# Four units of the next A pass scored ahead, and B's head in other banks

## The reference

```
x = x + attn_a(layernorm(x))   # 16 heads of 8, over the 256 positions, with a bias table by distance
x = x + ffn(layernorm(x))      # one shared expert, and 7 routed ones of which each token takes the best 2
x = x + attn_b(layernorm(x))   # 16 heads of 8, over the 32 sequences at one position, output projection
x = x + ffn(layernorm(x))      # same weights again
```

## Time and profile before

| | us |
|---|---|
| median of 3 runs | 2579.62 (2575.34 to 2588.03) |
| the profiled execution | 2579.83 |
| its span in the trace | 2578.0 |
| TensorE, VectorE, ScalarE, POOL busy | 2069.0, 1596.0, 1358.8, 881.0 |

### The profile page before, as it was taken

How to read it: one execution, slowest core, us unless ns; L and a number is a source line. 1 busy time by engine, 2 the same in 40 slices (tenths; PEclk the granted TensorE clock), 3 DMA queues, 4 the chain that set the end, 5 groups by cost and what they waited for, 6 DMA issues and landing times. The chain is left out here.

```text
span 2578.0 us, 51329 instructions
## 1 busy us (share of the span) xinstructions
PE 2069.0 (80%) x14166; PEld 1400.4 (54%) x14166; DVE 1596.0 (62%) x6106; ACT 1358.8 (53%) x2893; POOL 881.0 (34%) x953
## 2 busy tenths in 40 slices
PE   5789999999999999949999656767676676599995
PEld 3456666666666666626665444545545454366663
DVE  3477777777777777736555346565656655355552
ACT  3577888888888888715444332323223232154442
POOL 3111111111111111126777612222231313177776
PEclk8788888888888888869999867676777777699998
DMA  5100000000000000036777511101010100377774
GB/s 199 56 16 15 16 17 17 17 17 17 17 17 17 17 17 17 14 110 155 178 178 169 110 30 32 31 29 33 25 37 25 33 25 25 128 160 176 181 175 81
DMA packets 125947, 168.85 MB, mean 65 GB/s; under 512 B 17288, under 2 KB 93968, under 8 KB 125888
## 3 DMA queue, kind: packets, MB, share of 16 engines
q1 hardware_dynamic: 62400, 122.50, 15.0%
q0 software_dynamic: 51968, 37.26, 9.8%
q10 hardware_dynamic: 11520, 8.39, 1.2%
HBM read 111.96 MB, written 56.12 MB: 65 GB/s over the span
## 5 line engine op out<-in xcount | busy, mean ns | idle before, releaser
L1092 ACT ACTIVATE z<-z,nm 128x256 f32<-128x256 f32 x1024 | 440.2, 500 | 94.1 <-DVE nm L1342 93.8
L1342 DVE CUSTOM_DVE_ANT_0 z<-bank_S,big 128x256 f32<-128x256 f32 x1024 | 378.9, 420 | 166.8 <-PE bank_S L1615 127.8
L961 POOL DMA_INDIRECT sent<-rows,slots x256 | 249.2, 973 | 243.2 <-DVE slots L1425 167.1
L1502 DVE SCALAR_TENSOR_TENSOR both<-both,bank_E 128x512 f32<-128x512 f32 (+1 forms) x228 | 155.5, 682 | 227.1 <-ACT both L1162 226.7
L1031 POOL DMA_INDIRECT out_x<-yo,xs x152 | 236.1, 1553 | 119.8 <-ACT yo L1176 43.5
L1031 POOL DMA_INDIRECT x<-yo,xs x152 | 235.4, 1549 | 119.3 <-DMA x<-yo,xs 43.1
L946 POOL COPY seen<-seen 128x8 f32<-128x8 f32 x32 | 6.1, 189 | 720.2 <-DVE picked L1308 684.1
L1615 PE MATMUL bank_S<-kx,qx 32*128 32x256 f32 x1024 | 207.1, 363 | 34.8 <-DVE nm L1342 31.0
L1696 PE MATMUL bank_E<-xbh,w_gu 128*128 128x512 f32 (+1 forms) x342 | 182.3, 533 | 39.1 <-DMA w_gu<-w_split 26.5
L1615 PEld LDWEIGHTS bank_S<-kx,qx 32*128 32x128 f32 x1024 | 126.4, 207 | 118.3 <-DVE nm L1342 64.4
L1162 ACT ACTIVATE both<-bank_E 128x512 f32<-128x512 f32 (+1 forms) x228 | 137.8, 604 | 95.6 <-PE bank_E L1698 91.6
(11 more groups left out here) (215 smaller groups left out, 4421.5 us busy)
## 6 DMA issues: line engine op xcount, KB each, us to landing
w_gu<-w_split SPq DMA_DIRECT2D x76, 704.0 KB, 5.4
xs<-sent SPq DMA_DIRECT2D x76, 264.0 KB, 2.7
w_dn<-w_split SPq DMA_DIRECT2D x76, 192.0 KB, 5.3
w_split<-w_gu SPq DMA_DIRECT2D x7, 704.0 KB, 3.1
both<-in_w_raw SPq DMA_DIRECT2D x8, 544.0 KB, 4.7
xin<-in_x SPq DMA_DIRECT2D x16, 256.0 KB, 2.7
sent<-rows,slots POOLq DMA_INDIRECT x256
x<-xo ACTq DMA_DIRECT2D x16, 256.0 KB
```

Source lines behind the costliest of these rows:

```text
L961: pool.indirect_dma_start(out=sent, out_offset=bass.IndirectOffsetOnAxis(ap=slots[:, n:n + 1], axis=0), in_=rows[:, k, t, :], in_offset=No ...
L1092: last = act.activation(zt, zt, ACT.Exp, bias=nm[:, n % NM_RING, t:t + 1], scale=-1.0)
L1342: last = dve.tensor_tensor_reduce(z[:, n % Z_RING, t * SEQ:(t + 1) * SEQ], bank[s][:, t * SEQ:(t + 1) * SEQ], bias_a[:, h, P - P * t:P - P ...
L1502: dve.scalar_tensor_tensor(out=a, in0=a, scalar=1.0, in1=in_blocks(q)[0:m, :], op0=ALU.add, op1=ALU.mult).then_inc(ba_ready, 1)
```

## The change

Three things change together.

- `EARLY = 4`: `scores` and `probs` of units 0 to 3 of the pass `ahead` are now run in the body in which the pass is still ahead (`of_next`), and `following` runs units 4 to 31. The ring `probT` has 8 slots in place of 5. The first four units of pass 0 stand in `FIRST`.
- B's head uses banks of its own: `turn1` and `v` use E2, `qk` uses S1 and O. In a body E2 is used by turn1 of `ahead`, bturn of `following`, v of `ahead`; S1 and O by bscores of `following`, qk of `ahead`, bout of `following`. B uses Q0, Q1 and PY no more, so that `turn2`, `gate` and `up` don't wait for the head, and the head doesn't wait for `end`, `gate` and `up`.
- The needs are rewritten to match (`needs_unit`, `back`), and the scheduler treats a step of the next pass and the same step of this one as two sequences (`name = (s[0], of_next(kind, *s))`). Its rule, its weights and the durations in `WORK` stay.

```diff
-PT_RING = 5
+PT_RING = 8
+EARLY = 4
...
-        "B": {"S0": 3, "S1": 2, "T": 3, "O": 2, "E2": 1, "Q0": 1, "Q1": 1, **CHAIN}}
+        "B": {"S0": 3, "S1": 3, "T": 3, "O": 3, "E2": 3, "Q0": 0, "Q1": 0, "Y": CHAIN["Y"],
+              "PY": 0}}
+SCORED_IN = ("S0", "S1", "T", "O")
...
+def back(step, eng, n, by):
+    seen = (n - EARLY) % UNITS >= by
+    return (seen, (eng, step, (n - by) % UNITS))
...
+def needs_unit(eng, step, n):
+    if step == "scores":
+        if eng == "pe":
+            spreads = [(n < EARLY, ("act", "spread", n // 4 + k)) for k in range(2)] if n % 8 == 0 else []
+            return spreads + [back("scores", "dve", n, 2)]
+        if eng == "dve":
+            return [(True, ("pe", "scores", n)), back("probs", "pe", n, Z_RING)]
+        return [(True, ("dve", "scores", n))]
+    if eng == "pe":
+        return [(True, ("act", "scores", n)), back("probs", "act", n, 2)]
+    used = (n - PT_RING) % UNITS
+    return [(True, ("pe", "probs", n)), (n >= PT_RING or n < EARLY, ("pe", "mix", used // 4))]
...
     if step == "turn1":
-        return [("dve", "norm1", NORM_PARTS - 1), ("dve", "end", 0)] if eng == "pe" else [("pe", "turn1", 0)]
+        if eng == "act":
+            return [("pe", "turn1", 0)]
+        return [("dve", "norm1", NORM_PARTS - 1)] + ([("dve", "end", 0)] if kind == "A" else [])
     if step == "qk":
         if eng == "pe":
-            return [("act", "turn1", 0), ("dve", ("gate", "up")[n], FT - 1)]
+            return [("act", "turn1", 0), ("dve", "bscores", SCORED_IN.index(("S1", "O")[n])) if kind == "B"
+                    else ("dve", ("gate", "up")[n], FT - 1)]
...
     if step == "v":
-        return [("act", "turn1", 0)] if eng == "pe" else [("pe", "v", 0), ("pe", "bmix", TOK - 1)]
+        if eng == "pe":
+            return [("act", "turn1", 0), ("act", "bturn", 0)]
+        return [("pe", "v", 0), ("pe", "bmix", TOK - 1)]
...
     if step == "bout":
-        return [("act", "bturn", 0)] if eng == "pe" else [("pe", "bout", 0), ("pool", "keep", 0)]
+        if eng == "pe":
+            return [("act", "bturn", 0), ("act", "qk", 0), ("act", "qk", 1)]
+        return [("pe", "bout", 0), ("pool", "keep", 0)]
...
+def of_next(kind, step, n):
+    return step in AHEAD or kind == "A" and step in ("scores", "probs") and n < EARLY
...
-                    if s[0] not in seen and all(w in done for w in needs[t]):
+                    name = (s[0], of_next(kind, *s))
+                    if name not in seen and all(w in done for w in needs[t]):
...
+    B_HEAD = ("S1", "O")
...
-                src = bank[f"Q{n}"][:, :].rearrange("p (g b l) -> p g b l", g=GROUPS, b=TOK)
+                src = bank[s][:, :].rearrange("p (g b l) -> p g b l", g=GROUPS, b=TOK)
...
-                    pe.wait_ge(emptied["PY"], use(p.next(1) or p, "PY", 1))
+                    if p.kind == "A":
+                        pe.wait_ge(emptied["PY"], use(p.next(1) or p, "PY", 1))
                     turn_rows(p, xn2, "Y", 0)
...
-                    if n == 0:
+                    if n == 0 and p.kind == "A":
 
                         pe.wait_ge(emptied["Q0"], use(p.next(1) or p, "Q0", last_use(p, "Q0")))
```

More of the change, by code:

```diff
@@ L298, in needs_before @@
     if step in ("turn2", "twin", "keep") and eng in ("pe", "pool"):
-        return [("dve", "norm2", last)] + ([("dve" if kind == "A" else "act", "v", 0)] if step == "turn2" else [])
+        return [("dve", "norm2", last)] + ([("dve", "v", 0)] if step == "turn2" and kind == "A" else [])
     if step == "begin" and eng == "pool":
@@ L309, in needs_before @@
         ready = [("act", "qk", 0), ("act", "qk", 1)]
-    if step in ("gate", "up") and eng == "pe" and n == 0:
+    if step == "turn1" and eng == "pe" and kind == "B":
+        return [("act", "v", 0)]
+    if step in ("gate", "up") and eng == "pe" and n == 0 and kind == "A":
         return [ready[step == "up"]]
[L312 to L320, removed]
+    if step in ("scores", "probs"):
+        return [w for seen, w in needs_unit(eng, step, n) if not seen]
     if step == "mix" and n == 0 and eng == "pe":
-        return [("pool", "vmove", 0), ("dve", "context", 2 * GROUPS - 1)]
+        return [("pool", "vmove", 0), ("dve", "context", 2 * GROUPS - 1)] + [("act", "probs", 3)] * (EARLY > 3)
     if step == "v" and eng == "dve":
@@ L408, in order, with one_round @@
         free = {e: end - shift for e, end in free.items()}
-        out, done = one_round(everything, needs, before, earlier, free, work, chain, rule, total)
+        out, done = one_round(kind, everything, needs, before, earlier, free, work, chain, rule, total)
     return out
-def one_round(everything, needs, before, earlier, free, work, chain, rule, total):
+def one_round(kind, everything, needs, before, earlier, free, work, chain, rule, total):
     hand_over = rule["hand over"]
@@ L440, in one_round, with first_order @@
     return out, done
-FIRST = {k: order(k, steps_ahead(k), []) for k in "AB"}
+def first_order(kind):
+    steps = steps_ahead(kind)
+    head, units = ([x for x in steps if (x[0] in AHEAD) == w] for w in (True, False))
+    a, b = order(kind, head, []), order(kind, units, [])
+    return {e: a[e] + b[e] for e in FLOW}
+FIRST = {k: first_order(k) for k in "AB"}
 ALONE = {k: order(k, steps_attention(k, True), []) for k in "AB"}
@@ L708, in last_use, with early, late, of_scores @@
         return USES[p.kind][name] - 1
+    def early(p):
+        return 0 if p.first else -1
+    MID = 1
+    def late(p):
+        return 2 if p.last else 3
+    def of_scores(s):
+        return MID if s in B_HEAD else 0
+    def of_out(p, s):
+        return late(p) if s in B_HEAD else 2
     def cols(n):
@@ L1569, in attention @@
                     next_use(p, f"Q{n}", 0)
[L1570 to L1578, removed]
-                                                 tile_position=(0, 32 * a))
-                        last.then_inc(filled[f"Q{n}"], 1)
-                        return
                     pe.matmul(bank[f"Q{n}"][:, :], proj[:, half, n, :], xnT[:, :], start=True, stop=True
```

117 lines of the change are left out of this document (68 added, 49 removed).

## The result

The changed kernel takes 2541.8 us (median of four runs, 2536.7 to 2549.3) beside 2579.9 us for the kernel before on the same chip: ratio 0.985, 95% interval 0.982 to 0.989. That is 38 us faster and far from the 2403 forecast, outside its range too.

The account below looks back on a forecast made before the run. It took A to be bounded by three nearly full engines all stalling at the body boundary, B by a serial chain through its head. 2579.8 - 62 (A) - 113 (B) = 2405, stated as 2403 us; range 2348 to 2480, the forecast's own 2385 to 2430.

Parts of the forecast that it names:

- nothing is removed; 4 of 32 units move over the boundary: A loop: four units, 4.3 us of TensorE work, fill its 3.15 us of holes at the body boundary.
- 3.15 us of holes and 1.3 of clock: A loop: filled TensorE holes plus some returned clock shorten each body by 4.4 us, 62 us over 14 bodies.
- the clock's 5.1 us: A loop: what a whole return of the half-clock stretch to full clock would be worth per body.
- the clock returns in A: Rival for the A loop: full clock comes back, 7.3 us a body, 102 us, total 2365 us; chance 0.22.
- The very first pass: Start and end of A: first pass pays four units ahead of the loop, last saves them; 6 us at most.
- The rings cost nothing: A loop: the larger ring of turned probabilities adds no waits; if too small, bounded by one unit, 1.45 us.
- 8.1 us a body: B loop: freeing the head from the experts shortens bodies from 44.4 to 36.3 us, 113 us over 14 bodies.
- another chain takes over in B: Rival for the B loop: half the gain is lost, 4 us a body, 56 us, total 2462 us; chance 0.24.
- Cover exists: B loop: two widenings of 2.4 us each hide in 12 us before the additions, ScalarE idling 31 us a body.
- The list of what would show it wrong: TensorE waiting over 3 us at qk 1 or bout in B; norm2 behind early units, or half clock unshortened, in A.
- what would show it right: B: bodies of 34 to 38.5 us, early turn1 and qk, no VectorE hole near 9.75, longest hole before the additions.
- loops (a) and (b): B body: (a) attention, bscores to additions into h, 27.6 us; (b) experts, turn2 to norm2's last part, 30.9 us.

Follow-up runs that it names:

- e15: The kernel before with 64 idle VectorE instructions ahead of its A loop: 46 us slower than the kernel before, ratio 1.019.
- e3: The kernel before with 21 idle VectorE instructions ahead of its A loop, slower chip: 22 us slower than the kernel before.
- e4: The changed kernel with 105 idle VectorE instructions ahead of its A loop, slower chip: 0.960 of the kernel before.
- e6: The changed kernel with 105 idle VectorE instructions ahead of its A loop, chip like the first: 41 us faster than the changed kernel.
- e5: The changed kernel run again unaltered on a chip like the first: 41 us slower than e6.
- e13: The A part alone (B as before) with 105 idle VectorE instructions ahead of the A loop: 25 us faster than the kernel before, ratio 0.990.
- e16: The B part alone (no early units, ring of 5), chip like the first: 2530 us, 0.981 of the kernel before.
- e8: e6 with the third tanh and bturn's copy ahead of the second widening on ScalarE: 2454 us, 0.951 of the kernel before.
- e7: e6 with hand-written orders of the B loop body that put B's head early on TensorE, ScalarE and VectorE: 38 us faster than e6.
- e12: e8 with B's head moved forward a little on TensorE, ScalarE and VectorE, slower chip: 24 us slower than e8.
- e11: e8 run again unaltered on a slower chip: 2675.3 us, 0.950 of the kernel before.
- e14: e13 with two early units in place of four and 115 idle VectorE instructions: 54 us slower than the kernel before.
- e2: The B part alone (no early units, ring of 5), slower chip: 2789 us, 0.991 of the kernel before.

## Why the prediction was wrong

**A, the step "nothing is removed; 4 of 32 units move over the boundary".** It failed by what it left out: the moved units also stand ahead of the loop, which shifts VectorE's loop code by 21 instructions. The loop is 366 instructions of VectorE in the trace of the kernel before and 368 in the changed one, with those of its sequencer. The Trainium skill (Runtime: NRT & Kernel Launch, Instruction fetch mechanics) gives 512 instructions to 32 KiB, so 64 bytes each, and says that a taken branch to a target outside the pages held stalls on a fetch. By that I estimate the loop at 2.9 of the trace's 8 KB pieces (the page has blocks of 16 KiB; the packets measured here are 8 KB, and those decide), so that it lies across three or four. The packets bear the piece out: in a body of the changed kernel they start about 4, 14, 109, 230 and 350 instructions of VectorE behind the jump, and in e15, whose loop is shifted by 43 more, about 4, 14, 60, 191 and 320. Two come at the jump, and three, some 125 instructions apart, move with the loop. Whether a fourth piece of 8 KB or a third block of 16 KiB is what no longer fits, the four positions that ran don't tell. Here e3, e4, e6 and e15 agree with the rule: shifted by 21 or 64 it is fetched, by 0 or 126 (21 + 105) it isn't. Price: 41 us in the changed kernel (e5, e6), 46 in the one before (e15), 22 there on the slower chip with the smaller shift (e3). I had costed rings, waits and DMAs of the step, and no view of the kernel before could show the fetches; what it did show, the loop's length in instructions, I didn't count.

**A, 3.15 us of holes and 1.3 of clock.** The mechanism was right and the size nearly so: 64.8 to 61.4 us a body in e13, 3.4 against 4.4 (2.7 in e6, the same A code). The split was wrong: TensorE's holes fell by 5.73 - 4.26 = 1.5 us (from 59.10 busy of 64.83 to 57.14 of 61.40) and the clock gave 2.0. I took a quarter of the clock's 5.1 us; about two fifths came. So "the clock returns in A" was somewhat nearer than I allowed, and the reason I gave against it (turns and scores kept it low in the kernel before) held only in part: with no hole ahead of them the same turns and scores ran at the full clock at six boundaries of e13 (521.64 is one) and began at half at eight (462.19). By the Trainium skill's rule for transposes (TensorE: Matmul & The Clock Gate, Part 4: PE-mode transpose) no clock was to be won; e13 doesn't agree, since 5.5 us a body less were spent at half.

**"The very first pass ... taken as zero, 6 us at most".** In the changed kernel 3.6 us are left at the mark of the first body, within the bound but not zero, and the last pass saves nothing. In e13 that mark comes 15.5 us later (217.59 beside 202.09, with 105 idle instructions in it; the start varies by 3 us between runs), and the end of A is 3 us longer. So 13 x 3.4 = 45 us from the loop leave 26, and e13 measures 25. "The rings cost nothing" held: no wait for a ring slot shows in the A loops of the changed kernel and of e13.

**B, 8.1 us a body.** Measured 4.0 (44.3 to 40.3), 50 us for B alone (e16): the rival "another chain takes over in B", with its 4 us a body, to the letter, and its 56 us nearly. The step that failed is "Cover exists": ScalarE idles for 31 us of the body, but the widenings didn't fall into that. They came at 1901 to 1906, after 8.09 us of idling, since turn1 is turned only at 1896.04; and they stood ahead of bturn's copy, which I had listed as queued behind them without pricing it, and of the third tanh, which I hadn't listed. Undoing that one order gives 2.8 us of the 4.1 that were missing (e8). The list of what would show it wrong didn't catch this: TensorE doesn't wait at qk 1, waits 1.59 us for bturn's copy, under the 3 named, and VectorE waits for bout 4.23 us beside 3.86 before. Of what would show it right, one sign failed: VectorE's longest hole stands ahead of the third tanh's product (6.95 us) and not ahead of the additions. The last 1.3 us (37.6 against 36.3) no run gave: e7 and e8 meet at 37.6, and e12 is worse than e8. What sets 37.6 is argued, not shown: from turn2 on VectorE works for 20 us nearly without a hole, for both passes at once, and then tanh, down, bout and norm2 follow in series. My loops (a) and (b) were taken each by itself, and both pass through that one queue.

**The sum.** Forecast 62 for A and 113 for B. Found: 25 and 50, less 41 to 46 for the fetches. The size of A's and B's terms misses by 100 us, the fetches by 41. e8, the changed kernel with VectorE's loop placed well and two steps moved ahead of the second widening on ScalarE, is the best of all at 2454 us, 0.951 of before and 85 us under the changed kernel; the slower chip agrees (0.950, e11).

## What to carry to other kernels

Before costing a change that adds instructions ahead of a loop, count each engine's instructions in the loop and look at the instruction packets of the page in the stage of the loop: if any fall there, or a hole without a releaser stands where the loop jumps back, shift the loop by some idle instructions and measure. Idle time of an engine is cover for a long operation only if the operation is ready by then; look at what stands behind it in that queue, and move it behind the short ones that others wait for. Measure half of a cure before taking it for half of the gain: four units gave 25 us here (e13), and two, which left TensorE's hole at the boundary, cost 54 (e14), for a reason that stays open.

## What the runs showed of the hardware

VectorE fetched its loop of 366 to 368 instructions anew in every iteration, five packets of 8 KB and 2.5 us without work, when the loop was shifted by 21 or 64 instructions, and never when shifted by 0 or 126. B's loop of 153 or 154 instructions was never fetched anew. The same program took 2789 us on one chip and 2530 on another (e2, e16), TensorE busy for 2183 and 2046 us and the other engines alike: half-clock time in an A body of the same code was 27.1 us there (e2) and 13.7 here (e16). And half-clock time and the body's length go together: 8.1, 10.5, 13.6, 17.1 and 20.4 us at half belong to bodies of 61.4, 62.2, 64.8, 68.3 and 68.2 us (e13, e6, before, e15, e14); which of the two brings the other, these figures alone don't tell.
